# AdaLN attention and expert block: the mask turned behind the first attention group, high parts ahead of weight copies, filling products in the first step

## The reference

```python
h = layernorm(x) * (1 + ca) + sa
x = x + ga * attention(h)        # 16 heads of 8; K = exp(-sigma*|k_i - q_j|^2), no normalisation; out = K @ v, then Wproj
h = layernorm(x) * (1 + cb) + sb
x = x + gb * experts(h)          # 8 experts of 128x128, sum over the 2 with the largest router logits
```

## Time and profile before

| | |
|---|---|
| median of 3 runs | 225.71 us (224.12, 225.71, 226.25) |
| profiled execution | 226.44 us, of which the span from first to last instruction is 224.6 us |
| mean granted TensorE clock | 0.992 |
| PE busy | 210.0 us, 93% of the span |
| DVE, ACT, POOL busy | 174.8 us (78%), 163.5 us (73%), 137.3 us (61%) |
| PE's share of the chain that ended last | 69%; DVE 18% |

### The profile page before, as it was taken

One profiled execution on the slowest core, in us unless ns is written; L12 is line 12 of the kernel. 1 busy time (PEld: TensorE's weight loads), 2 busy tenths in 40 slices (PEclk: granted clock), 3 DMA queues, 4 the chain that ended last, 5 costly groups with the idle time before them and its releaser, 6 DMA issues.

```text
span 224.6 us, 8205 instructions
## 1 busy us (share of the span) xinstructions
PE 210.0 (93%) x3240; PEld 150.1 (67%) x3240; DVE 174.8 (78%) x610; ACT 163.5 (73%) x234; POOL 137.3 (61%) x204
## 2 busy tenths in 40 slices
PE   7986888899999999999999999999999999999993
PEld 7653444577776767777677767676776776766792
DVE  4775441868888897988897888979888988787884
ACT  5228688877786868798777878686978777777362
POOL 5455547474866757575849577675757594435183
PEclk9997899999999999999999999999999999999999
DMA  5562424332423333434333243324242323300001
GB/s 149 149 206 99 146 87 121 117 109 84 120 85 115 95 136 86 146 90 146 92 125 93 78 128 103 118 77 149 88 148 69 140 62 107 99 23 26 3 23 48
DMA packets 22472, 22.94 MB, mean 102 GB/s; under 512 B 2330, under 2 KB 20258, under 8 KB 22434
## 3 DMA queue, kind: packets, MB, share of 16 engines
q1 hardware_dynamic: 21962, 21.79, 30.6%
q10 hardware_dynamic: 472, 0.62, 0.8%
HBM read 6.65 MB, written 2.12 MB: 39 GB/s over the span
## 4 chain that ended last, share of the span: by engine, by line
PE 69%; DVE 18%; issue 4%; DMA 3%; ACT 2%; SPq 1%; POOL 1%; POOLq 0%; ACTq 0%
PE att_ps L981 25%; PE qkv_ps L1000 8%; PE scores L961 7%; DVE acc L708 5%; DVE eq L787 4%; PE qkv_ps L1119 3%; PE qkv_ps L1009 3%; DMA st<-norm_parts 3%; PE scores L913 2%; DVE topi L784 2%; PE mid_ps L1083 2%; DVE x_all L746 2%; ACT probs L495 2%; PE qkv_ps L1121 2%; PE qkv_ps L1120 2%
## 5 line engine op out<-in xcount | busy, mean ns | idle before, releaser
L495 ACT ACTIVATE probs<-scores 128x1024 f32<-128x1024 f32 x128 | 124.3, 1022 | 12.8 <-PE scores L961 7.7
L981 PE MATMUL att_ps<-probs,vpad 128*32 128x256 f32 x1024 | 69.1, 386 | 0.0
L981 PEld LDWEIGHTS att_ps<-probs,vpad 128*32 128x32 f32 x1024 | 31.4, 110 | 16.9 <-issue 1.0
L961 PE MATMUL scores<-st 32*128 32x256 f32 x512 | 37.7, 331 | 4.6 <-ACT probs L495 2.7
L368 POOL TENSOR_TENSOR ve<-stats,eps 128x2 f32<-128x2 f32 x32 | 6.2, 193 | 43.4 <-DVE stats L688 43.4
L961 PEld LDWEIGHTS scores<-st 32*128 32x128 f32 x512 | 23.3, 184 | 13.8 <-ACT probs L495 4.7
L708 DVE SCALAR_TENSOR_TENSOR acc<-ffn_ps,mask,acc 128x128 f32<-128x128 f32 x114 | 32.0, 342 | 0.2
L411 POOL TENSOR_TENSOR sq<-qkf 128x512 f32<-128x512 f32 x15 | 15.6, 1040 | 24.6 <-DVE qkf L714 24.6
L375 POOL TENSOR_SCALAR xn<-x_all,stats,rstd 128x128 f32<-128x128 f32 x30 | 25.5, 853 | 1.6
L708 DVE SCALAR_TENSOR_TENSOR acc<-qkv_ps,mask,acc 128x128 f32<-128x128 f32 x64 | 18.0, 344 | 9.5 <-PE qkv_ps L1121 9.5
L370 POOL TENSOR_TENSOR rstd<-ve,expo 128x2 f32<-128x2 f32 x32 | 22.6, 707 | 2.5
(11 more groups left out here) (170 smaller groups left out, 428.5 us busy)
## 6 DMA issues: line engine op xcount, KB each, us to landing
st<-hl SPq DMA_DIRECT2D x47, 256.0 KB
rb_all<-rb_rows SPq DMA_DIRECT2D x16, 192.0 KB, 3.2
out_dram<-x_all SPq DMA_DIRECT2D x16, 128.0 KB, 1.9
x_all<-in_L_attn_x_dram SPq DMA_DIRECT2D x13, 128.0 KB, 3.2
st<-norm_parts SPq DMA_DIRECT2D x60, 16.0 KB
we_sb<-in_L_ffn_w_experts_dram SPq DMA_DIRECT2D x1, 512.0 KB, 5.8
w_mod_sb<-in_L_wmod_dram SPq DMA_DIRECT2D x1, 256.0 KB, 5.1
st<-hl ACTq DMA_DIRECT2D x1, 256.0 KB
```

The lines of the kernel that those rows point to most:

```text
L495: nc.scalar.activation(probs[:, g, 2 * half:2 * half + 2, :], scores[:, 2 * half:2 * half + 2, :], ACT.Exp, scale=two_sigma).then_inc((exp ...
L961: i = pe.matmul(scores[:, r, t * T:(t + 1) * T], st[rows, par, g, t * P:(t + 1) * P], st[rows, par, g, T:2 * T], start=True, stop=True)
L981: i = pe.matmul(att_ps[r * ROWS:(r + 1) * ROWS, 0:T], heads[:, g * ROWS:(g + 1) * ROWS], probs[:, g, r, t * T:(t + 1) * T], start=(g == 0 ...
```

## The change

Three edits. In every step PE's list has `pv(k, 0)` ahead of `turn_mask(k - 2)` instead of behind it. On DVE, batch 1's `high_parts` goes from the head of step 0 (behind the second half of `expert_weights`, two copies) to directly behind `queries_keys(1)`. And in step 0 PE gets five filling products into the bank `att_ps`: three behind `qk_scores(0, 1)`, with a wait for a copy out of that bank, and two behind `norms(1)`.

```diff
@@ DVE, step(k)
                     expert_weights(0)
                     queries_keys(1)
+                    high_parts(1)
                     expert_weights(1)
                     return
...
                 if has(k + 1):
                     if k > 0:
                         queries_keys(k + 1)
-                    high_parts(k + 1)
+                        high_parts(k + 1)
@@ PE
-            def warm_up(n, w=P):
+            def warm_up(n, w=P, bank=None):
                 for _ in range(n):
-                    pe.matmul(scores[:, R - 1, 0:w], ident[:, :], ident[:, 0:w], start=True, stop=True)
+                    pe.matmul(scores[:, R - 1, 0:w] if bank is None else bank[:, 0:w], ident[:, :], ident[:, 0:w], start=True, stop=True)
@@ PE, step(k)
                 qk_scores(k, 1)
+                if k == 0:
+                    pe.wait_ge(wr_sb_ok, 1)
+                    warm_up(3, P, att_ps)
...
                 if has(k + 1):
                     norms(k + 1)
+                if k == 0:
+                    warm_up(2, P, att_ps)
                 qk_scores(k, 2)
+                pv(k, 0)
                 if has(k - 2):
                     turn_mask(k - 2)
-                pv(k, 0)
                 if has(k + 1):
                     values(k + 1)
                 pv(k, 1)
```

## The result

The changed kernel took 222.71 us as a median (222.32, 222.43, 222.99, 223.40), beside 225.20 for the kernel before on the same chip: a ratio of 0.9895, with a 95% interval of 0.9851 to 0.9939. A second, later series of twelve executions of the same kernel gave 223.41 and a ratio of 0.9908 (0.9870 to 0.9945). So it is faster by about 1%, at the edge of what I had called measurable. The forecast was 222.0 with a range of 220.6 to 224.3; the time is in the range, and near the price of one of the rivals (B, 222.8). The narrower range that the prediction's terms gave by themselves, 221.0 to 223.3, holds the first median and misses the second by 0.1.

What follows compares the result with a forecast made beforehand. PE was taken to bound the kernel, through waits for DVE's residual and a low clock at the start; 2.3 + 1.5 = 3.8 us off the profiled 226.44, with the median 0.7 lower, gave 222.0, range 220.6 to 224.3.

Steps and rivals of the forecast that it cites:

- B: Start: the kernel before doesn't lose clock in every execution; without the fall high parts gain 0.6, giving 222.8; chance 0.10.
- Part 1, the loop: Loop: the new order fills PE's wait for DVE's residual, 0.20 us per step, 2.3 us in all.
- The passage cost: Loop, PE: pv and on to a full-width product takes 1.00 us, 0.14 more than pv in front of values.
- The four margins: Loop: pv(k, 0) for bank att_ps, turn_mask with mask_rows, experts(k - 2, 0) and turn_x keep enough room, 0.2 us gained holds.
- The margin behind `mask_rows`: Loop, DVE: later mask_rows is covered up to 0.45; it would decide only from a turn_mask some 0.9 us later.
- Part 2, the start: Step 0: earlier high parts and filling products bring the first scores of step 1 forward by 1.5 us.
- Everything of step 1 hangs on them through `queries_keys(2)`: Step 1: all follows its first scores through queries_keys(2), POOL and seven transfers, so the 1.5 us stay.
- I expect the clock to stay at its upper level: Step 0: with filling, PE is busy about 2.1 instead of 1.03 of the 2.80 us up to 20.2, keeping its clock up.
- a granted clock of 0.50 near 20: Start: the sign in the profile that would make rival A right.
- rival A: Start: PE's clock falls all the same, so only the loop's 2.3 us are gained, 223.4; chance 0.13.
- The sum: Whole kernel: 2.3 from the loop and 1.5 from the start, 3.8 us off; forecast 222.0.

Runs made afterwards that it cites:

- e7_turn_split: The changed kernel with one of turn_mask's two transposes behind pv(k, 0) and the other behind values(k + 1); 226.86 us, ratio 1.0066.
- e2_start_only: The changed kernel with the loop's order of before, so only high parts moved and five filling products; 225.00 us, ratio 0.9979.
- after_again: The changed kernel as it is, run once more in a later series of twelve executions; 223.41 us, ratio 0.9908.
- e12_split_after_rows: The changed kernel, with DVE's split of the expert weights in step 0 waiting for POOL's normalised rows of batch 2; 222.32 us, ratio 0.9817.
- e1_order_only: The kernel before with only the order of pv(k, 0) and turn_mask changed; 222.65 us, ratio 0.9861.
- e3_order_high: The changed kernel without its five filling products; 222.77 us, ratio 0.9880.

## Why the prediction was right or wrong

- **Part 1, the loop.** Right in mechanism and nearly in size: 0.17 us per step measured, 0.20 worked out, 2.0 us instead of 2.3 in all. The passage cost was right too (1.00 from pv to the transpose, and 0.12 to 0.14 measured by itself in e7_turn_split). The stretch from the third scores to `values` came out at 1.66, with 1.67 forecast; some 0.04 per step is lost ahead of it.
- **The four margins.** All held. `pv(k, 0)` started right behind the scores in every step, so the bank `att_ps` cost nothing; `turn_x` and `experts(k - 2, 0)` wait for nobody from step 2 on (in step 1 `turn_x` waits 0.47 for POOL's rows). The margin behind `mask_rows` was less than the 0.9 that I gave it: 0.44 later costs nothing, 0.73 later costs some 0.07 per step.
- **Part 2, the start: the term that failed.** The 1.5 us were counted from an execution with the fall, and e2_start_only gave 0.8 by its median (225.00 against 225.83), with 1.1 as the upper end. Two steps failed. The first is the clock, in the next point. The second is "Everything of step 1 hangs on them through `queries_keys(2)`". Up to the fourth scores every number held, where the clock did, but those products also wait for POOL's normalised rows through `turn_x(2)` and ACT. I had those rows' end, and didn't ask what DVE does when PE hands it `values(1)` earlier. It starts the split of the expert weights, and the two engines' work at the same time stretches the rows from 1.58 to 2.91 us. In after_again the products were 1.06 earlier than before and not 1.5; with the split moved behind the rows, in e12_split_after_rows, 1.50.
- **At the upper clock.** There the prediction's figure for the start was B's 0.6, and 224.63 against 224.52 is none of it. The kernel before has the faster PE too in such executions, so it may meet the same stretched rows, and then both kernels are bound by them; no such execution of it was profiled, and this is not shown.
- **The clock.** "I expect the clock to stay at its upper level" was wrong in the profiled execution: it fell about 17.5, just ahead of the filling, which then ran at the lower clock on the path. By the prediction's own sign, a granted clock of 0.50 near 20, rival A was right there, and its price of 223.4 is that execution's 223.40. Over many executions rival B was right: the kernel before has executions without the fall, 20 of 63, and the changed kernel some with it, 7 of 16. The Trainium skill's rule (TensorE: Matmul & The Clock Gate, "What's actually happening") that a change of clock falls differently from run to run is what the traces show: the products begun at 7.30 took 1.87 us in one and 1.04 in another, and the granted clock was 0.50 from 17.5 on in the changed kernel's first trace, from 19.5 in e1_order_only's, from 20.2 before, and from 26.6 in after_again's.
- **The sum.** 2.0 + 0 is 2.0 us at equal clock; the medians differ by 2.5 and 2.4 in the two series, the rest through the share of executions with a fall. With 3.8 forecast, the time is in the range by part 1 and by the range's width; that it came within 0.7 us of the forecast was partly luck, since the median beside it, 225.20, was also 0.5 below the 225.71 that I started from. The chance of 0.75 for faster by over 1% was too high for what turned out to be 1% itself, and B's 0.10 too low.

What stays open: how much the five filling products keep the clock up (below 0.996 are 19 of 57 executions with them and 43 of 63 of the kernel before, but also only 4 of 12 of e1_order_only and e3_order_high, which have none), and how the start of e12_split_after_rows would do without them; that kernel was not run.

## What to carry to other kernels

When an engine's wait is filled, check what the engines that it releases will start earlier and what that runs beside: here 0.44 of the 1.5 us that PE had gained were lost at a stretched operation of POOL, because DVE's split began earlier with PE, and one wait in the right place took them back. A cover for a moved operation is the time until its reader's next reader is late, and it is found by moving the operation a place further, not only by reading idle times. With a clock that falls in some executions, compare executions at equal mean clock, and don't spend products to keep it up where they can stand on the path.

## What the runs showed of the hardware

DVE and POOL slow each other in these traces. POOL's two operations of 128x128 took 1.58 us by themselves and 2.91 beside DVE's copy and subtraction of 128x1024 (0.73 and 1.22). When DVE's pair ran beside POOL's addition of 128x256 instead, the pair took 0.88 and 1.63 and the addition 1.17, which takes 0.72 by itself (e12_split_after_rows and after_again). The Trainium skill has this as a rule (SBUF — State Buffer, "Terms"): DVE and GpSimd take turns on one pair of ports, and the one that loses stands until the other's instruction is through. The traces agree that the two are in each other's way, and only in part that the one stands throughout: 1.33 us were lost beside 1.95 us of DVE's work. Beside the subtraction POOL's second operation took 1.79 instead of 0.79, so that 1.00 of 1.13 us was lost; beside the copy of 0.73 its first one took 1.13, and lost 0.34.

The clock fell although PE never stood for longer than 1.3 us at a time in the 6 us ahead of the fall (1.24 at most in the kernel before, 1.21 in the changed one), and the executions of the kernel before that lie below 0.996 take 1.6 us longer than the others (226.10 against 224.52). The initial rise seems to move as well: the same products, begun at 7.30, took 1.87 us in one execution and 1.04 in another.

Going over from products on 32-wide strips to one over the full width costs PE 0.12 to 0.14 us each time (0.58 against 0.46 and 0.44, and 1.00 against 0.86).
